# A fused attention and ternary FFN block on one core: weighing ahead of q, a sum in PSUM, weight sums moved

## What is computed

```python
def _bi_wkv(r, k, v, w, u, time_emb):        # here v = k
    tf = sigmoid(sum(time_emb))
    decay = exp(-exp(w)) * (0.5 + 0.5 * tf)
    ek = exp(minimum(k, 30)); ekv = ek * v
    nf, df = scan(a * decay + ekv_t), scan(b * decay + ek_t)      # forward in time
    nb, db = the same scans, reversed in time
    euk = exp(minimum(u + k, 30))
    num = nf + nb - ekv + euk * v
    den = df + db - ek + euk
    return sigmoid(r) * (num / maximum(den, 1e-8)) * (0.8 + 0.2 * tf)

x = x + attention(_bi_wkv(x, fside, fside, w, u, cond))   # 16 heads of 16, causal softmax, w_qkv, w_out
x = x + ffn(_bi_wkv(x, fside, fside, w2, u2, cond))
# ffn: silu(x @ up) * (x @ gate) @ down, each weight rounded to -1, 0, 1 times mean(|W|)
```

## Time and profile before

| | us |
|---|---|
| median of 3 runs | 175.5 (175.47 to 176.79) |
| the profiled execution | 175.76 |
| its span | 173.9 |
| busy: PE, DVE, ACT, POOL | 146.8, 147.5, 115.5, 54.8 |

### The profile page before, as it was taken

One profiled execution on the slowest core, in us unless ns is written; L12 is line 12 of the kernel. 1 busy time (PEld: TensorE's weight loads), 2 busy tenths in 40 slices (PEclk: granted clock), 3 DMA queues, 4 the chain that ended last, 5 costly groups with the idle time before them and its releaser, 6 DMA issues.

```text
span 173.9 us, 3854 instructions
## 1 busy us (share of the span) xinstructions
PE 146.8 (84%) x1558; PEld 97.7 (56%) x1558; DVE 147.5 (85%) x255; ACT 115.5 (66%) x184; POOL 54.8 (32%) x57
## 2 busy tenths in 40 slices
PE   0007897977999799999999899999998999998992
PEld 0007882333378457754675567536855675787781
DVE  0599998999999999999958999994689999575673
ACT  2557976989877566598657354985572547886560
POOL 8800052999930086521000655310002232000000
PEclk9999999999999999999999999999999999999998
DMA  4899413505001323645630065347310000010001
GB/s 105 343 432 424 175 62 121 107 19 115 9 2 60 124 55 66 121 80 99 161 135 19 6 121 105 77 80 188 102 61 0 0 8 0 4 64 0 4 2 60
DMA packets 7290, 16.15 MB, mean 93 GB/s; under 512 B 936, under 2 KB 4456, under 8 KB 6888
## 3 DMA queue, kind: packets, MB, share of 16 engines
q1 hardware_dynamic: 5544, 10.52, 16.0%
q0 software_dynamic: 1440, 5.24, 15.3%
q10 hardware_dynamic: 288, 0.14, 0.4%
HBM read 6.43 MB, written 1.05 MB: 43 GB/s over the span
## 4 chain that ended last, share of the span: by engine, by line
PE 36%; DVE 23%; issue 6%; ACT 4%; POOL 2%; POOLq 1%; DVEq 0%; ACTq 0%
DVE row_max L711 7%; PE attn_ps L1144 7%; PE acc_ps L1068 4%; PE attn_ps L1039 3%; PE wide L1222 3%; PE wide L1117 2%; PE attn_ps L1234 2%; DVE hid L779 2%; PE wide L1122 2%; PE acc_ps L1004 2%; PE turn_ps L1004 2%; POOL hid_lo L296 2%; PE attn_ps L1186 2%; DVE x_hi L730 1%; PE turn_ps L1199 1%
## 5 line engine op out<-in xcount | busy, mean ns | idle before, releaser
L267 POOL TENSOR_TENSOR extra<-extra,k_t 128x512 f32<-128x512 f32 x7 | 10.0, 1426 | 62.4 <-DVE x_lo L736 43.4
L711 DVE TENSOR_REDUCE row_max<-wide 128x4 f32<-128x1024 f32 (+1 forms) x24 | 28.7, 1214 | 0.6 <-PE wide L1097 0.6
L428 ACT ACTIVATE probs<-wide 128x1024 f32<-128x1024 f32 x24 | 23.8, 1018 | 2.9 <-PE wide L1122 1.9
L466 ACT ACTIVATE silu<-attn_ps,up_scale 128x256 f32<-128x256 f32 x24 | 11.2, 473 | 21.4 <-PE attn_ps L1039 21.4
L624 DVE TENSOR_TENSOR_SCAN fwd<-decay,ek 128x256 f32<-128x256 f32 x32 | 23.1, 768 | 0.0
L636 DVE TENSOR_TENSOR_SCAN bwd<-ek,decay 128x255 f32<-128x255 f32 x32 | 20.2, 678 | 0.0
L1242 PE MATMUL wide<-ones 128*128 128x128 f32 x24 | 5.3, 421 | 14.0 <-DVE fwd L827 14.0
L296 POOL TENSOR_TENSOR hid_lo<-hid,hid_hi 128x512 f16<-128x512 f32 x9 | 11.1, 1239 | 15.0 <-ACT hid_hi L473 15.0
L1039 PE MATMUL attn_ps<-x_hi,w_tern 128*128 128x256 f16 x96 | 14.3, 274 | 1.1 <-DVE x_hi L730 1.0
L1039 PE MATMUL attn_ps<-x_lo,w_tern 128*128 128x256 f16 x96 | 13.9, 273 | 1.2 <-DVE x_lo L736 1.2
L1144 PE MATMUL attn_ps<-probs,v_pad 128*32 128x256 f32 (+1 forms) x192 | 12.6, 334 | 0.7 <-ACT probs L428 0.6
(11 more groups left out here) (156 smaller groups left out, 339.0 us busy)
## 6 DMA issues: line engine op xcount, KB each, us to landing
stack<-halves SPq DMA_DIRECT2D x24, 128.0 KB, 2.1
fwd<-extra POOLq DMA_DIRECT2D x5, 512.0 KB, 4.8
fwd<-bwd POOLq DMA_DIRECT2D x5, 512.0 KB, 4.4
w_raw<-wup_d SPq DMA_DIRECT2D x1, 1024.0 KB, 11.5
w_raw<-wgate_d SPq DMA_DIRECT2D x1, 1024.0 KB, 13.2
w_raw<-wdown_d SPq DMA_DIRECT2D x1, 1024.0 KB, 14.9
wqkv<-wqkv_d SPq DMA_DIRECT2D x1, 768.0 KB, 7.2
k_t<-k_d SPq DMA_DIRECT2D x1, 768.0 KB, 8.6
```

Source lines behind the costliest of these rows:

```text
L428: nc.scalar.activation(probs[:, j, :], flat(wide[j % 2][:, :, :]), ACT.Exp, scale=SOFTMAX_SCALE).then_inc(prob_done, 1)
L466: nc.scalar.activation(silu[:, e % 2], up, ACT.Silu, scale=up_scale[:, 0:1]).then_inc(silu_done, 1)
L711: nc.vector.tensor_reduce(out, src, AX.X, ALU.max).then_inc(max_done, 1)
```

## The change

1. Batch 0's first gate is summed by TensorE: each term is multiplied with the identity and accumulated in `wide[0]` (denominator in the first bank, numerator in the second). `extra` goes in first. VectorE clamps the denominator out of PSUM and gates the numerator out of PSUM. `ones` matmuls stand between.
2. `high_halves(0, 1)` and `high_halves(0, 0)` come ahead of the second and third pass of absolute weights. The matmul that totals the sums follows `scores(0, 0)`, and VectorE takes the first maximum before it makes `w_scale`.
3. q's projection goes to two different banks (`q_bank`: one in `acc_ps`, one in `wide[0]`), and its halves are signalled tile by tile; SP copies them tile by tile (four copies of half the size), and one full copy is issued by GpSimd (batch 0) or ScalarE.
4. For b = 1 and 2, `weigh` 4 and 5 come ahead of q's projection of b + 1, `row_reciprocals`, `normalize` and `second_wkv` ahead of q's halves, `values` behind `project`.
5. In the tail, `tail_project(0)` comes ahead of `tail_score_t(5)`, `first_reciprocal` ahead of `exp_probs` 4, `tail_sigmoid` ahead of `exp_probs` 5, and `tail_project(1)` ahead of the last low half of `tail_up_gate`.

```diff
+        def wait_stacks(engine, n):
+
+            engine.wait_ge(second_in, 16)
+            engine.wait_ge(stack_in, 16 * (8 * n - 1))
+
+        def second_high(engine, b):
+            engine.wait_ge(zeros_q, 2)
+            engine.wait_ge(hi_done[0], CT * (b + 1))
+            if b >= 2:
+                engine.wait_ge(score_t_done, NT * (b - 1))
+            engine.dma_start(stacks[b % 2][2::4, 0, :, :], halves[:, 0, 0, :, :]).then_inc(stack_in if b else second_in, 16)
+
+
+        q_bank = (acc_ps[:, 0, :], wide[0][:, 0, 0:T])
...
+                sp.wait_ge(hi_done[1], b + 1)
+                for r, parts in enumerate(SPREAD):
+                    if parts[1] == 0:
+                        sp.dma_start(stack[r::4, 1, :, :], halves[:, 1, 0, :, :]).then_inc(stack_in, 16)
+                sp.wait_ge(lo_done[1], b + 1)
+                for r, parts in enumerate(SPREAD):
+                    if parts[1] == 1:
+                        sp.dma_start(stack[r::4, 1, :, :], halves[:, 1, 1, :, :]).then_inc(stack_in, 16)
+                for part, done in enumerate((hi_done[0], lo_done[0])):
+                    for ct in range(CT):
+                        sp.wait_ge(done, CT * b + ct + 1)
+                        sp.dma_start(stack[part::4, 0, ct::CT, :], halves[:, 0, part, ct, :]).then_inc(stack_in, 16)
...
-            pool.wait_ge(hi_done[0], 1)
+            second_high(pool, 0)
...
+            def high_keys(b):
+                act.wait_ge(qk_done[1], b + 1)
                 if b:
-                    act.wait_ge(stack_in, 32 * len(SPREAD) * b)
+                    wait_stacks(act, b)
                 for ct in range(CT):
-                    hi = nc.scalar.activation(halves[:, side, 0, ct, :], bank[:, ct, :], ACT.Identity,
-                                              bias=vec[:, bias + ct:bias + ct + 1])
-                hi.then_inc(hi_done[side], 1)
+                    hi = nc.scalar.activation(halves[:, 1, 0, ct, :], turn_ps[:, ct, :], ACT.Identity,
+                                              bias=vec[:, V_BK + ct:V_BK + ct + 1])
+                hi.then_inc(hi_done[1], 1)
+
+            def high_queries(b):
+                act.wait_ge(qk_done[0], b + 1)
+                if b:
+                    wait_stacks(act, b)
+                for ct in range(CT):
+                    nc.scalar.activation(halves[:, 0, 0, ct, :], q_bank[ct], ACT.Identity,
+                                         bias=vec[:, V_BQ + ct:V_BQ + ct + 1]).then_inc(hi_done[0], 1)
+                if b:
+                    second_high(act, b)
...
                     act.wait_ge(abs_done, i)
                 nc.scalar.activation(w_tern[i][:, :], w_raw[i][:, :], ACT.Abs,
                                      accum_out=abs_sum[:, i:i + 1]).then_inc(abs_done, 1)
-                if i == 1:
-                    high_halves(0, 1)
+                if i == 0:
+                    high_keys(0)
                     extra_exp(0, 1)
-                    high_halves(0, 0)
+                    high_queries(0)
             copy_values(0)
 
...
                 more, f = b + 1 < B, b - 1
                 if b:
                     if b > 1:
-                        row_reciprocals(f)
                         extra_exp(1, b)
-                        copy_values(b)
                     nc.scalar.preload_act_table(ACT.Silu)
                     tanh_x1(f)
-                    if b == 1:
-                        copy_values(b)
+                    copy_values(b)
                     if more:
                         sigmoid_x_by_tanh(b + 1)
...
                     if not more:
                         tail_row_reciprocals(0)
+                    if not more:
+                        first_reciprocal(1, b)
                     exp_probs(b, 4)
                     if more:
-                        high_halves(b + 1, 1)
+                        high_keys(b + 1)
                     else:
-                        first_reciprocal(1, b)
+                        tail_sigmoid()
                     exp_probs(b, 5)
                     if more:
                         first_reciprocal(1, b)
-                        high_halves(b + 1, 0)
+                        row_reciprocals(b)
+                        high_queries(b + 1)
...
+            def first_gate_by_tensor():
+
+                forward(0, 0, 1)
+                backward(0, 0, 1)
+                forward(0, 0, 0)
+                dve.wait_ge(sum_ps_done, 1)
+                nc.vector.tensor_scalar(fwd[0][:, 1, :], wide[0][:, 0, :], DEN_MIN, None,
+                                        ALU.max).then_inc(den_done[0], 1)
+                backward(0, 0, 0)
+                refine(0, 0)
+                dve.wait_ge(sigx_done, 1)
+                dve.wait_ge(sum_ps_done, 2)
+                nc.vector.tensor_tensor(fwd[0][:, 0, :], wide[0][:, 1, :], sig_x[:, 0],
+                                        ALU.mult).then_inc(numsig_done, 1)
+                first_wkv(0)
...
                     else:
                         backward(1, b + 1, 1)
-                    low_halves(b + 1, 0)
                     refine(1, b)
+                    normalize(b)
+                    second_wkv(b)
+                    low_queries(b + 1)
+                    if b + 2 < B:
+                        backward(0, b + 2, 0)
+                    else:
+                        backward(1, b + 1, 0)
                 else:
+                    maxima(0, 0)
                     dve.wait_ge(abs_total, 1)
...
+                banks = (q_bank, (turn_ps[:, 0, :], turn_ps[:, 1, :]))[side]
+                if side == 0 and b:
+                    pe.wait_ge(prob_done, NT * (b - 1) + 5)
                 if side == 1:
                     pe.wait_ge(wkv1_done, b + 1)
...
+            def add_to_sum(half, term, start=False, stop=False):
+                mm = nc.tensor.matmul(wide[0][:, 1 - half, :], identity[:, :], term[:, half, :],
+                                      start=start, stop=stop, skip_group_check=True)
+                if stop:
+                    mm.then_inc(sum_ps_done, 1)
+
+            def warm(n):
+                for _ in range(n):
+                    nc.tensor.matmul(wide[1][:, 0, 0:P], ones[:, :], ones[:, :], start=True, stop=True)
+
+            pe.wait_ge(ident_made, 2)
+            pe.wait_ge(ex_done[0], 1)
+            add_to_sum(1, extra[0], start=True)
+            pe.wait_ge(prod_done[0], 1)
+            add_to_sum(0, extra[0], start=True)
+            warm(2)
+            pe.wait_ge(fwd_done[0], 2)
+            add_to_sum(1, fwd[0])
+            pe.wait_ge(bwd_done[0], 2)
+            add_to_sum(1, bwd[0], stop=True)
+            pe.wait_ge(fwd_done[0], 4)
+            add_to_sum(0, fwd[0])
+            warm(1)
+            pe.wait_ge(bwd_done[0], 4)
+            add_to_sum(0, bwd[0], stop=True)
+            warm(3)
             pe.wait_ge(recn_done[0], 1)
-            for _ in range(3):
-                nc.tensor.matmul(wide[0][:, 0, 0:P], ones[:, :], ones[:, :], start=True, stop=True)
+            warm(2)
...
                 if b:
-                    if b > 1:
-                        values(b)
                     project(f)
-                    if b == 1:
-                        values(b)
+                    values(b)
...
-                    pe.wait_ge(abs_done, 3)
-                    pe.wait_ge(lo_done[0], 1)
-                    nc.tensor.matmul(acc_ps[:, 0, 0:3], ones[:, :], abs_sum[:, :], start=True,
-                                     stop=True).then_inc(abs_total, 1)
                     keep_busy(3, attn_ps[:, 1, :])
                     for j in range(NT):
                         scores(0, j)
+                        if j == 0:
+                            pe.wait_ge(abs_done, 3)
+                            pe.wait_ge(lo_done[0], CT)
+                            nc.tensor.matmul(acc_ps[:, 0, 0:3], ones[:, :], abs_sum[:, :], start=True,
+                                             stop=True).then_inc(abs_total, 1)
                         keep_busy(1, attn_ps[:, 1, :])
...
                     for j in range(2, NT):
+                        if j == NT - 1:
+                            tail_project(0)
                         tail_score_t(j)
                         if j < NT - 1:
                             tail_weigh(j - 2)
-                    tail_project(0)
                     for j in range(NT - 3, NT):
                         tail_weigh(j)
                     continue
...
                 score_t(b, 5)
                 weigh(b, 3)
-                queries_or_keys(b + 1, 0)
                 weigh(b, 4)
                 weigh(b, 5)
-
-            for part in range(2):
-                for e in range(2):
-                    tail_up_gate(e, (0,), part)
+                queries_or_keys(b + 1, 0)
+
+            for e in range(2):
+                tail_up_gate(e, (0,), 0)
+            tail_up_gate(0, (0,), 1)
             tail_project(1)
+            tail_up_gate(1, (0,), 1)
```

86 lines of the change are left out of this document (37 added, 49 removed).

## The result

The changed kernel takes 180.04 us (median of 4, 179.69 to 180.21) against 175.49 for the kernel before in the same comparison: a ratio of 1.0235 [1.0197, 1.0273] with its 95% interval, slower. The profiled execution took 180.06 with a span of 178.2, 4.3 longer than the 173.9 before. The forecast was 176.3, its range 174.4 to 178.0. It was wrong.

A forecast was written before the change was run, and what follows sets the result against it. The prediction took a chain of waits passing between TensorE and VectorE to bound the kernel. Its terms, +1.0 - 0.7 + 0.45 = +0.75 us, gave 176.3 us against the 175.5 median, range 174.4 to 178.0.

The forecast's parts named there:

- stretch (b): Batch 0 up to its maxima: stack copies, first scores, weight scaling; ScalarE, not the maxima, nearly ends it.
- Part 1: Head: batch 0's gate summed in PSUM by TensorE, clamp at 0.69 from PSUM; `wkv1` earlier by 0.75, say 0.8.
- g: How much earlier `wkv1` comes in the head: 0.75, say 0.8; ends -0.4 and 2.3.
- Part 2: Batch 0's stack copies and weight sums: late `w_inv` puts `neg_max` +1.6 later, the projection of heads' residual +1.0.
- rival C: Stack's half copies go by bytes: batch 0's scores 1.0 earlier, boundaries -0.65 each, 174.7 us; chance 0.20.
- The step that failed: Behind batch 0's `neg_max`: its copy, transposed scores, weighing and batch 1's projections follow, moving the heads' projection by 1.6.
- The absorbed 0.6: Before batch 0's residual: VectorE's own work hides 0.6 of the 1.6 delay, leaving +1.0.
- Part 3: Boundaries behind b = 1 and 2: weighing ahead of q gains -0.35 each, -0.7 for two, the stack being last.
- Part 4: Tail: the last `exp_probs` now stands behind the sigmoid, so weighing 5 and everything after wait; +0.45.
- B: Head: TensorE stays at its lower level through the denominator's sum, g = -0.4; slower, 177.5 to 178.1 us; chance 0.20.

The follow-up runs named there:

- before_early: Kernel before, with GpSimd's 512 KB accumulating transfer of batch 0 moved earlier, between the two passes of `bound_sums`; 178.09 us, 1.0145.
- full_both: `full` with both the weights' total and the tail back in the order of the kernel before; 174.48 us, 0.9931.
- warm_early: `full_both` plus 16 more TensorE filler matmuls at the very start, once the ones tile exists; 173.71 us, 0.9881.
- full_sums: `full` with the total of absolute weights back ahead of the first scores and first maximum; 175.26 us, 0.9969.
- hold: Changed kernel, with GpSimd's 512 KB transfer of batch 0 held until the copy of `neg_max` has landed; 176.28 us, 1.0044.
- hold_neg: Changed kernel, with GpSimd's 512 KB transfer of batch 0 released by `neg_max` itself, not by its copy's landing; 175.91 us, 1.0013.
- busy: Changed kernel, transfer not held, with more TensorE fillers ahead of batch 0's first scores, turn of maxima and transposed scores; 178.42 us, 1.0184.
- part3_back: `full_both` with q's projection and values at the boundaries back in the order of the kernel before, stack copies still split; 175.58 us, 0.9998.
- full: Changed kernel with GpSimd's transfer held and fillers ahead of first scores (15), turn of maxima (5) and transposed scores (12); 176.03 us, 1.0005.
- fill_late: Changed kernel with held transfer and extra fillers only ahead of the turn of maxima and the transposed scores; 176.42 us, 1.0049.

## Why the prediction was wrong, step by step

**What bounds the kernel.** Right for the edits themselves; what cost the 4.5 us was a wait that no edit touches. Of stretch (b) I had read ScalarE, SP, TensorE and VectorE, and not GpSimd.

**Part 1.** The mechanism was right, and so was the clamp's 0.69 from PSUM. g was mis-sized: 2.05 instead of 0.8, since the level rose near 11 and not at 13.1, and the clamp waited 0.50 instead of 1.5. About 0.3 of the 2.05 is not the change's: VectorE started at 9.37 for 9.68, as it did in `before_early`, which has the old head and `wkv1` at 19.39. Both moments occur: `wkv1` lay between 17.40 and 19.04 in the 13 profiles of kernels with this head, so the value taken and its upper end describe the scatter, and the mean (18.15) makes g 1.5. Behind it stands a rule of the Trainium skill, "TensorE: Matmul & The Clock Gate" (section "What's actually happening"): how many matmuls run at the lower level varies from run to run of one kernel. The traces agree (the `fwd` term at 1.02 in one and 1.67 in another). The same section of the Trainium skill puts the cost below 1% of a typical kernel. That agrees too, and is still enough to decide a comparison of this size: `wkv1` moved by 1.64 of 176 us, 0.9%, and the medians of `full_both` and `warm_early` lie 0.77 apart.

**Part 2, up to `neg_max`.** Right. SP's half copies cost 0.63 each (2.54 for four), so rival C fell, and GpSimd's copy landed 2.2 us after its issue, well ahead of SP's last. With the measured g the forecast's own sum puts the first scores at 27.45 and `neg_max` at some 37.6; they are at 27.48 and 37.76. The wait for `w_inv` is there (2.52), and `full_sums` shows its cost.

**The step that failed** is the sentence behind it: "Behind it stand SP's copy of it, the transposed scores, weighing, and k's and q's projections of batch 1", moved "by 1.6". It carried two things over from the trace before without a row: that the copy of `neg_max` still lands 1.85 after its issue, and that TensorE still works at the full level behind it. The first cost 2.70 (`hold`, `hold_neg` and `before_early` show it), the second 1.8 at the projection of heads (`busy` shows it). The first could have been asked of the profile before: GpSimd's transfer was issued 2.1 us behind the copy (39.77 for 37.69), its stretch hangs on the first scores, which the forecast itself moved forward, while it moved `neg_max` back. By the forecast's own numbers they close 0.26 + 1.6 of the 2.1. In the trace they close 2.32: GpSimd's stretch begins 1.30 earlier and is 0.57 shorter, and the copy is issued 0.45 later. That was near enough to put up a rival with its price, 2 to 3 us, from the earlier trace rows, where a 512 KB transfer takes 4.4. I gave that row a use for the wrong copy. The second could not be read from a profile at 1.00; only the price of the lower level stood there (0.445 for 0.28), and no rival used it behind the head.

**The absorbed 0.6** was 0.70, but 0.46 of it came back before the first low half, most of it (0.37) since the scores of batch 1 wait for the stack. The forecast priced the copies for batch 0 and behind b = 1 and 2, and put them at nothing, without a reason, at the boundary behind b = 0. **Part 3**: -0.35 a boundary, measured -0.44 and -0.41, and 0.40 in `part3_back`; the stack was last, as forecast (98.78, released by the stack's copies), and `row_rec` came 2.07 earlier within the batch for 1.9. **Part 4**: +0.45, measured +0.40, by the named chain.

**Luck.** `full`, which has neither the collision nor the fall of the clock, took 176.03, near the forecast's 176.3. So the sum of the forecast's own terms came out, but partly by luck: a g of 1.5 for 0.8 is set off by the 0.46 of the first boundary and by a tail that cost 0.4 to 0.8.

**The rivals.** None names what happened. B ended on this side, but by another mechanism and too low. The range's upper end, 178.0, took in only rivals built of the diff's own waits; no case let a transfer that the diff doesn't touch change its place.

Why TensorE's clock falls at 38.3 of the changed kernel's profile and not in that of the kernel before, with the same gap of 1.22 us ahead of the turn of the maxima, stays open. That it stayed at 1.00 in the profiles with enough fillers in the later gaps is shown (`busy`, `full` and its relatives, `fill_late`), not what tips it.

## What to carry to other kernels

When an edit moves one engine forward and another back, list every transfer that either releases, those that the diff doesn't touch too, and look whether two of them change places; a small one that the critical path waits for should be issued first, or the large one should wait for it. Price a stretch of TensorE at both levels of its clock, and where work on it is on the path early in a kernel, try fillers on it from the first moment on. An edit that looks like a loss may hide a gain: with one wait more the change that cost 2.4% here is even with the kernel before (1.0013, 1.0044), and it gives 1.2% once TensorE is kept at work too, from the start on, and the weights' total and the tail stay where they were.
